# A second adder whose units are partly added in pairs on VectorE before TensorE sums them

## The reference, cut to what matters

```python
def adder2d(x, w, stride=1, padding=0):
    """AdderNet L1-distance conv: out[n,co,ho,wo] = -sum_{ci,kh,kw} |x_patch - w[co,ci,kh,kw]|."""
    ...
    for kh in range(K):
        for kw in range(K):
            xs = xp[:, :, kh:kh + Ho * stride:stride, kw:kw + Wo * stride:stride]
            diff = jnp.abs(xs[:, None] - w[None, :, :, kh, kw, None, None])
            acc = acc - diff.sum(axis=2)
    return acc

    identity = x
    out = conv2d(x, w_shift1, stride=1, padding=0)
    out = adder2d(out, w_add1, stride=1, padding=0)
    out = jax.nn.relu(batchnorm(out, bn1_gamma, bn1_beta, bn1_mean, bn1_var))
    out = conv2d(out, w_shift2, stride=1, padding=1)
    out = adder2d(out, w_add2, stride=1, padding=1)
    out = jax.nn.relu(batchnorm(out, bn2_gamma, bn2_beta, bn2_mean, bn2_var))
    return jax.nn.relu(out + identity)
```

## Time and profile before

| | us |
|---|---|
| median of 3 runs | 411.81 |
| lowest and highest | 409.03, 412.48 |
| the profiled execution | 407.41 |
| its span in the profile | 405.3 |
| TensorE busy | 353.4 (87%) |
| VectorE busy | 216.5 (53%) |
| ScalarE busy | 166.4 (41%) |
| GpSimd busy | 14.2 (4%) |

### The profile page before, as it was taken

The page is one execution under the profiler, slowest core; times in us unless marked ns, Lnnn a source line. Parts: engine busy times, 40 slices in busy tenths (PEclk is TensorE's granted clock), DMA queues, the critical chain, the costliest instruction groups (busy, mean ns, idle before and its releaser), DMA issues.

```text
span 405.3 us, 11365 instructions
## 1 busy us (share of the span) xinstructions
PE 353.4 (87%) x5061; PEld 196.0 (48%) x5061; DVE 216.5 (53%) x278; ACT 166.4 (41%) x158; POOL 14.2 (4%) x30
## 2 busy tenths in 40 slices
PE   4898399999999996787559999586799999999996
PEld 3534135763333343663123334353586666677774
DVE  1583968999999995656990042436511112111212
ACT  2374668887899942221006665322211111111110
POOL 3034000000000002000000000000000000000000
PEclk9889779999999999999999999969999999999999
DMA  4119300000000008000000000000000000000001
GB/s 151 23 33 349 139 0 2 2 2 2 2 2 2 2 2 309 22 16 0 2 0 2 2 2 2 0 0 2 0 2 3 3 3 3 3 3 3 3 3 41
DMA packets 9767, 11.57 MB, mean 29 GB/s; under 512 B 3894, under 2 KB 8888, under 8 KB 9720
## 3 DMA queue, kind: packets, MB, share of 16 engines
q1 hardware_dynamic: 9352, 9.55, 7.1%
q0 software_dynamic: 224, 1.10, 0.7%
q10 hardware_dynamic: 144, 0.20, 0.1%
HBM read 10.44 MB, written 0.40 MB: 27 GB/s over the span
## 4 chain that ended last, share of the span: by engine, by line
PE 62%; DVE 24%; issue 6%; DMA 2%; ACT 2%; SPq 1%; DVEq 1%; ACTq 0%
PE PS L846 62%; DVE pool_ L707 9%; DVE TOPS L761 4%; DMA PAR<-in_par 1%; DVE TMP L679 1%; DMA W1R<-in_fwa 1%; DVE RSC L493 1%; SPq L214 1%; DVE pool_ L794 1%; DMA W4R<-in_aw 1%; DVE pool_ L531 0%; DVE ASEG L629 0%; DVE MSC L624 0%; DVE TMP L491 0%; DVEq L762 0%
## 5 line engine op out<-in xcount | busy, mean ns | idle before, releaser
L846 PE MATMUL PS<-pool_,CON 128*32 128x392 f32 (+2 forms) x1392 | 121.3, 502 | 0.9 <-DVE pool_ L707 0.6
L374 ACT ACTIVATE pool_<-TMP,WA 128x3136 f32<-128x3136 f32 x27 | 78.4, 2931 | 18.8 <-PE PS L846 15.3
L707 DVE TENSOR_SCALAR pool_<-TMP,WA 128x3136 f32<-128x3136 f32 x45 | 81.7, 1847 | 5.5 <-PE PS L846 5.3
L846 PEld LDWEIGHTS PS<-pool_,CON 128*32 128x32 f32 (+1 forms) x1392 | 52.6, 112 | 65.9 <-issue 51.9
L835 DVE COPY pool_<-PS 128x392 f32<-128x392 f32 x32 | 18.1, 567 | 84.0 <-PE PS L846 84.0
L459 ACT ACTIVATE pool_<-PS 128x392 f32<-128x392 f32 x32 | 15.9, 498 | 85.8 <-PE PS L846 85.8
L846 PE MATMUL PS<-pool_,WS 128*32 128x136 f32 (+3 forms) x1024 | 46.3, 333 | 0.0
L846 PE MATMUL PS<-HE,WS 128*32 128x136 f32 (+3 forms) x1024 | 46.3, 333 | 0.0
L846 PEld LDWEIGHTS PS<-pool_,WS 128*32 128x32 f32 x1024 | 31.5, 110 | 15.3 <-issue 9.8
L846 PEld LDWEIGHTS PS<-HE,WS 128*32 128x32 f32 x1024 | 31.2, 111 | 15.7 <-issue 10.2
L846 PE MATMUL PS<-CON 128*128 128x196 f32 (+1 forms) x142 | 28.9, 348 | 1.6 <-DVE TOPS L761 0.8
(11 more groups left out here) (202 smaller groups left out, 282.9 us busy)
## 6 DMA issues: line engine op xcount, KB each, us to landing
pool_<-in_pho SPq DMA_DIRECT2D x1, 3144.0 KB, 10.6
HE<-in_phe SPq DMA_DIRECT2D x1, 3136.0 KB, 14.0
CW<-in_cw SPq DMA_DIRECT2D x2, 576.0 KB, 4.5
CON<-in_con POOLq DMA_DIRECT2D x1, 732.5 KB, 5.9
out_y<-Y SPq DMA_DIRECT2D x1, 392.0 KB, 2.4
CON<-in_con POOLq DMA_DIRECT2D x1, 337.0 KB, 3.5
CQ<-in_ws SPq DMA_DIRECT2D x16, 9.0 KB
MPP<-in_mpp SPq DMA_DIRECT2D x1, 256.0 KB, 2.6
```

The costliest lines, as they stand in the source:

```text
L374: a.activation(RING[:, g % RG, :, :].rearrange("p b (r c) -> p b r c", r=SIDE), window(n // CQ), ACT.Abs, bias=WA2[:, n:n + 1], scale=-1.0 ...
L707: v.tensor_scalar(RING[:, g % RG, :, :].rearrange("p b (r c) -> p b r c", r=SIDE), window(n // CQ), WA2[:, n:n + 1], None, ALU.max).then_i ...
L846: return t.matmul(out_, lhsT, rhs, start=start, stop=stop, skip_group_check=True)
```

## The change

A pair is the unit n1 with c8 = 5 of an even tap (n1 = 5, 21, 37, 53) and the same channel of the next tap, n1 + 8 (13, 29, 45, 61). Both are VectorE's, and both go to the same output channel. The unit n1 is left out at its own place. At the place of n1 + 8 VectorE writes unit n1 into the ring slot with the tensor_scalar, waits on the new semaphore `pair_half`, and then adds max(x, w) of the second unit onto it with four scalar_tensor_tensor instructions, one for each image, 784 elements each, in place. TensorE then sums one group for both. The list `UNITS` holds the 68 places that are left, and ring slots and waits go by the position m in it; the work at set values of n stays at its n.

```diff
+PAIRED = 5
+FIRST = [CQ * tap + PAIRED for tap in (0, 2, 4, 6)]
+UNITS = [n for n in range(9 * CQ) if n not in FIRST]
+NG = CQ + len(UNITS)
+ON_ACT = [on_scalar(c8) for c8 in range(CQ)] + [on_scalar(n % CQ) for n in UNITS]
...
@@ VectorE (ScalarE's and TensorE's loops go over UNITS in the same way)
-            for n in range(9 * CQ):
-                g = CQ + n
+            for m, n in enumerate(UNITS):
+                g = CQ + m
...
                 if not ON_ACT[g]:
                     v.wait_ge(s["ring_free"], g - RG + 1)
-                    v.tensor_scalar(RING[:, g % RG, :, :].rearrange("p b (r c) -> p b r c", r=SIDE), window(n // CQ),
-                                    WA2[:, n:n + 1], None, ALU.max).then_inc(s["dve_unit"], 1)
+                    unit = RING[:, g % RG, :, :].rearrange("p b (r c) -> p b r c", r=SIDE)
+                    if n - CQ in FIRST:
+                        n1 = n - CQ
+                        v.tensor_scalar(unit, window(n1 // CQ), WA2[:, n1:n1 + 1], None, ALU.max).then_inc(s["pair_half"], 1)
+                        v.wait_ge(s["pair_half"], FIRST.index(n1) + 1)
+                        for b in range(NIMG):
+                            last = v.scalar_tensor_tensor(unit[:, b, :, :], window(n // CQ)[:, b, :, :], WA2[:, n:n + 1], unit[:, b, :, :],
+                                                          ALU.max, ALU.add)
+                        last.then_inc(s["dve_unit"], 1)
+                    else:
+                        v.tensor_scalar(unit, window(n // CQ), WA2[:, n:n + 1], None, ALU.max).then_inc(s["dve_unit"], 1)
...
@@ TensorE
-            def group(g):
+            def group(g, c8):
...
-                        last = mm(PS[32 * b:32 * b + 32, 6 + h, 0:HT], SEL[ON_ACT[g]][:, g % CQ, :], half(RING[:, g % RG, b, :], h), False, False)
+                        last = mm(PS[32 * b:32 * b + 32, 6 + h, 0:HT], SEL[ON_ACT[g]][:, c8, :], half(RING[:, g % RG, b, :], h), False, False)
```

More of the change, by code:

```diff
@@ L64 @@
 CQ = 8
-NG = CQ + 9 * CQ
-ON_ACT = [on_scalar(g % CQ) for g in range(NG)]
+PAIRED = 5
[3 more added lines that the diff above has]
+ON_ACT = [on_scalar(c8) for c8 in range(CQ)] + [on_scalar(n % CQ) for n in UNITS]
 ACT_UPTO = [sum(ON_ACT[:g]) for g in range(NG + 1)]
@@ L196, in build @@
             "sp_woke idle_src corr_in ws_rep x_low_in x_in par_in con_in wa1_in w_a_in sum_in mask_in ws2_in cw_in strip_in mst_in "
-            "ln_mean ln_cent ln_sq ln_var ln_sd ln_rs ln_bc ln_out con_head "
+            "pair_half ln_mean ln_cent ln_sq ln_var ln_sd ln_rs ln_bc ln_out con_head "
             "bn_sd bn_ready bn_chain pads zeroed c1_done y1_ready ring_free dve_unit act_unit adder_done "
@@ L907, in _ @@
             for g in range(CQ):
-                group(g)
+                group(g, g)
             mm(PS[0:1, 5, 500:501], CON[:, 0:1], CON[:, 0:1]).then_inc(s["adder_done"], 1)
@@ L935, in _ @@
                     mm(PS[:, 1, 0:2], con_("ones", P, 1), WRW[0:1, :]).then_inc(s["wmx_bc"], 1)
-                group(CQ + n)
+                group(CQ + m, n % CQ)
             t.wait_ge(s["xs9_ready"], 1)
```

## The result

The changed kernel takes 417.38 us (median of 4 runs, 415.95 to 418.32) against 410.52 before (409.03 to 412.48): the ratio is 1.0203, with a 95% interval of 1.0151 to 1.0256, so it is slower by 6.2 to 10.5 us; whether by more or less than 2% is not settled. (A ratio here comes from comparing executions and is not the quotient of the two medians; that is 1.0167, inside the interval.) The forecast was 418.4 us. The two profiled executions lie 10.2 us apart in their spans (415.5 and 405.3).

A forecast was written before the change was run, and what follows sets the result against it. VectorE, without slack from n = 23 on, was taken to bound the adder: +0.17 and +7.52 made 7.69 us, less 1.08 of slack +6.6, put on the median 411.81 for 418.4 us; range 413.8 to 422.8.

The forecast's parts named there:

- What bounds: In the second adder, TensorE and VectorE both full from 80.0 to 129.6 us; VectorE has about no slack from 79.88 on.
- The price of a pair: On VectorE, one tensor_scalar, a wait and four adds take 5.44 us against 1.76 for a plain unit: +3.68.
- the add's 0.89: Each 128x784 add on VectorE was taken as 0.89 us, from a tensor_tensor of that shape; bounds -0.09 to +0.09.
- Up to n = 23: Early adder: first pair starts 1.33 us sooner; idle and the missing n = 21 absorb most, leaving +0.17 us at n = 23.
- From n = 23 to the last unit: Three pairs (+11.04 us) less two units (3.52) add 7.52 on VectorE; the last unit ends 7.69 later.
- At the end: Behind the adder's last unit: 7.69 us less 1.08 of slack, so the sum starts 6.6 us later.
- rival 1: TensorE's clock falls during a pair's wait; +1.3 us at the last pair, up to +3.5; time 419.7 to 421.9; chance 0.22.
- the slack of 1.08 us: VectorE's wait for ScalarE before the sum behind the adder, expected to absorb 1.08 us of the delay.
- the prediction's own signs: Profile after: right if adds about 0.97 us, VectorE about 7 us busier; wrong if slot waits after n = 23 or lower clock.
- rival 2: In the adder, TensorE sets the pace and the adds fit VectorE's gaps: 406.5 us, faster; chance 0.03.
- rival 4: The pairs' adds on VectorE run at half rate, 12.8 us more: 431.2 us; chance 0.04.
- rival 3: The pairs' adds run at two elements a cycle, about 0.49 us each, shift +0.2: 412.0 us; chance 0.04.

The follow-up runs named there:

- e2_groups_back: Changed kernel plus eight zero-weight matmuls of a group's shape on TensorE before each pair's wait, restoring 72 groups' worth; 416.15 us, ratio to before 1.0138.
- e3_left_out: Only the removal: units n = 5, 21, 37, 53 left out on VectorE and TensorE, nothing added at n + 8; 401.23 us, ratio to before 0.9784.
- e6_immediate: Changed kernel with the adds' scalar a constant 0.0 instead of a weight column; adds 969 ns instead of 1030, n = 13 to sum 94.23 us.
- e1_warm: Changed kernel plus six unused matmuls on constants before TensorE's wait at each of the three later pairs; 417.40 us, ratio to before 1.0186.
- e4_adds_alone: Kernel before, all 72 units and groups kept, plus the wait and four adds at n = 13, 29, 45, 61; 425.07 us, ratio 1.0337.
- e8_last_pair: Changed kernel with only the last pair (n = 53 and 61), other units plain, 71 groups; single time 409.12 us.

## Why the prediction was right

**What bounds.** It was read rightly from the stretches: both engines full, VectorE with nothing left from n = 23 on. e2_groups_back and e3_left_out show the two sides of it: with the adds, TensorE's four groups are worth nothing; without the adds, the four units less on both engines are worth 6.7 us of the stretch, and TensorE then has no idle left.

**The price of a pair.** Forecast 5.44 us, measured 5.68, +3.92 over the plain unit instead of +3.68. The mis-sized term is the add's 0.89; it took (3.87 - 1.03) / 3 = 0.95. The nearest row was chosen by shape and kind; that it has a column as scalar, worth 0.06 us, was left out, and e6_immediate shows that this is all of it.

**Up to n = 23.** Forecast +0.17, measured 79.88 in both, so -0.32 counted from the first unit. The pair started 17.50 us behind the first unit, 1.88 sooner than n = 13 before (19.38), where 1.33 was forecast. The other 0.55 is luck: TensorE's clock, at 0.50 since the idle in front of the adder, came back about 6.8 us behind the first unit here and about 8.0 behind it in the profiled execution of before. In the seven kernels without n = 5 the stretch varies from 17.50 to 18.34, and in the same order as the time of the clock's return, 6.8 to 8.6 us. With both clocks back at the same time the shift of the sum would have been about 8.8.

**From n = 23 to the last unit.** 3 x 3.92 - 2 x 1.76 = 8.24, and 0.21 of waiting for a slot behind the clock's fall. The last unit started at 152.98, against 144.52 before (142.75 given in the timeline of before for two units, plus 1.77): counted from the first unit +8.1, where 7.69 was forecast.

**At the end.** Here the forecast's own sum failed, and rival 1 had it: the slack of 1.08 us was to be eaten. It was not; the sum waited 1.19 us for ScalarE, because TensorE's last 11 groups took 1.7 us longer at the fallen clock. Shift of the sum +8.26 instead of +6.6; without the fall, +7.0 (e1_warm). So the profiled execution went by rival 1, whose price of 1.3 us is 1.4 in e1_warm and e2_groups_back. The chance of 0.22 looks low: the clock fell after each of the three waits here, and over the four kernels with an unfilled wait of 2.2 to 2.4 us at the last pair it fell there in two (the changed kernel and e4_adds_alone, not e6_immediate and e8_last_pair). One execution of each does not give a rate. Of the prediction's own signs, two of the wrong ones came: a granted clock under 1.00 between 90 and 165 us (rival 1), and a wait of 0.21 us for a slot, though this was the clock's and not rival 2's. The adds of 1.03 us and 8.6 us more of VectorE's busy time were near the 0.97 and 7 named, and TensorE's waits of 2.79, 2.87 and 2.27 near the 2.8. Not seen at all was that the norm behind the adder may lose 0.6 to 1.0 us in the same way.

**The time.** 418.4 was forecast and 417.38 measured. The forecast's shift was 6.6 us; the medians are 6.9 apart, the ratio of 1.0203 gives 8.3, the profiled spans are 10.2 apart. The direction, the size and the mechanism were right, but that the median came within 1.0 us is partly luck, by the base: the profiled execution of before, 407.41 us, lies below all the runs shown, so the sum from its trace was put on a median 4.4 us higher, and that median itself came out 1.3 us lower with one more run. From the profiled execution the sum gives 414.0, and the profiled execution of the changed kernel took 417.34. The spans, 10.2 apart, show where the rest lies: 1.7 us in the adder (0.7 for the adds' price, 1.2 for the wait in place of the eaten slack, 0.2 for the slot, less 0.5 ahead of n = 23), 0.8 in the norm, 0.3 ahead of the adder and 0.8 in the 243 us behind. Rivals 2 to 4 are out: an add of half rate (rival 4) or double rate (rival 3) was not seen, and TensorE did not set the pace (rival 2).

## What to carry to other kernels

Before work is moved from the engine that has 62% of the chain to the one that has 24%, read both engines' busy time stretch by stretch: where both are full, the exchange rate decides, and here 2.2 us of VectorE (net of the unit left out) bought 1.3 us of TensorE. Doing each half of such a change alone (the removal without the addition, and the addition without the removal) gives the exchange rate directly, and one size in between gives the point of balance. A unit that takes three times as long as its neighbours, in a ring of five slots, also makes the consumer wait in one piece, and such a piece can cost TensorE its clock on top.

## What the runs showed of the hardware that was not expected

- **Whether the clock falls after a wait of 2 to 3.5 us is not told by the wait's length.** In the adder, TensorE's waits of 2.27, 2.34, 2.40, 2.79, 2.87 and 4.09 us were followed by a fall to 0.50, those of 2.17, 2.41, 2.54, 3.03 and 3.42 were not, and none of 1.77 or less was. Two rows show the pair of cases: at 118 to 122 us of e6_immediate, behind a wait of 3.42 us, and at the last pair of the changed kernel, behind 2.27 us (above, 0.50).

```profile
118.54 6.83 PE L858 MATMUL PS<-pool_,CON 128*32 128x392 f32 x80 [3.42 <-DVE pool_ L716]
...
118.00:120.00 2.00, 1.46 (x20) 0.66 (x24) 2.00 (x3) 0.10 (x1) 0.00 (x0) 1.00 0.00 0
120.00:122.00 2.00, 2.00 (x32) 0.79 (x26) 2.00 (x3) 1.05 (x2) 0.00 (x0) 1.00 0.04 8
```

- The same holds behind the adder, where TensorE is idle for 1.97 to 2.26 us in all ten profiled executions: in five the granted clock stayed at 1.00 behind it and the stretch from the sum to the first choice took 9.41 or 9.42 us, in the other five the clock fell to 0.50 and the stretch took 10.05 to 10.41. Which of the two comes was not settled by the length of the idle (1.97 in the kernel before without the fall, 1.97 in the changed one with it).
- A column of weights as the scalar of a VectorE instruction with two SBUF tensor inputs costs 0.06 us more than a constant (1030 against 969 ns at 128x784), the same as the 626 against 567 ns at 128x392 in the kernel before. That cost was in the trace that the prediction was made from, on a row that it did not use.
